# GpSimd adds the two bias rows of output projection and cross attention to the residual rows, in place of VectorE

## The chip, the cores and the metric

One Trainium2 chip, one of its cores. The time is the device time of one launch in microseconds (us); of several runs the median counts.

## The reference, cut to what matters

A decoder of two layers on x, 8 sequences of 256 rows of 256 numbers (fp32). Around the change, in the second layer:

```
x = x + L1_attn_ref(layernorm(x), ...)     # state-space mixer: ... return y @ out_proj_w.T + out_proj_b
x = x + L1_xattn_ref(layernorm(x), ctx)    # cross attention, 8 heads: ... return out @ Wo + bo
x = x + L1_ffn_ref(layernorm(x), ...)      # experts, top 2 of 8
```

out_proj_b and bo are rows of 256 numbers, the same for every row of x. The kernel holds them as `r_out` and `r_xo`, spread over the 128 partitions.

## The kernel before, in words

The 2048 rows lie in four pairs of sequences; a pair is 512 rows, four tiles of 128 rows by 256 numbers. `xst` holds the residual rows of all pairs in SBUF, so the rows of one pair are 128 partitions by 1024 numbers. Every engine runs a queue of its own, in the order in which it is written, and the queues meet at semaphores: `wait_ge` waits, `then_inc` counts up when an instruction is done. `hold` is a wait followed by a semaphore instruction.

After the first layer the function `mixer(p, q, n)` is called six times by `ssm_and_cross` (L157), once per step of a software pipeline over the pairs: n is the pair whose head (similarity, gates and projections up to the step sizes of the state space) is worked on, p the pair in the state space, q the pair in cross attention. The six calls are named M0 to M5 here: M0 is (None, None, 0), M1 (0, None, 1), M2 (1, 0, 2), M3 (2, 1, 3), M4 (3, 2, None), M5 (None, 3, None). M2 and M3 are the two turns of a hardware loop.

Inside one call VectorE's queue is (L1536 to L1593): the first drive product (L1483), then 32 units, each with a scan (L1493), the next unit's drive product (L1483), a piece of the head of pair n and of the cross attention of pair q, and the product that TensorE sums (L1501). Behind the units comes what is called the end here: products with the gate (L1551, L1552), the convolution of pair n (L1510, L1512), then

- the projection of pair p is added to its residual rows from PSUM, in two halves (L1567), and `r_out` is added to the pair's four tiles at once (L1569, counted by `xc_ready`), then the statistics of these rows (L1354, L1357); GpSimd turns the variance into 1/sqrt (L556, L557), and VectorE scales the rows (L1363, counted by `xn_ready`);
- between them the last tile of cross attention of pair q is added (L1474), and `r_xo` is added to the pair's four tiles at once (L1575); the statistics and the scaling of these rows follow, into `xr` (counted by `xr_ready`);
- the step sizes of pair n: the positive part from PSUM (L1585), and `step_sizes` (L1521 to L1534), which wait for ScalarE's absolute values (L994) and exponentials (L998). The last four-unit product L1534 is what the first drive product of the next call waits for.

GpSimd's queue in `mixer` (L644 to L668): the 1/sqrt of each normalisation, a copy of `xr` into `hst` (L663) once `xr_ready` has come, and, once the second half of the step sizes is there (`dt_ready`, L1532), three small memsets of the decay tiles (L668), for which the first drive product also waits (`starts_ready`). GpSimd does larger additions in the first layer too: L597 adds a bias row to a pair, 128x1024, the same shape as the additions above.

SyncE waits for `xc_ready` of all pairs (L528) before it loads the token numbers and the first expert weights. The first tile of cross attention in a pair waits for `xc_ready` as well (L1473).

The quoted lines, from VectorE's queue:

```
v.tensor_tensor(half, proj_banks[s][:, :].rearrange(...), half, ALU.add).then_inc(proj_added, 1)                 # L1567
v.tensor_tensor(pair, pair, wide(r_out, TT), ALU.add).then_inc(xc_ready, 1)                                      # L1569
step.apart(v.tensor_tensor(xst[:, ts(q, TT), :], xst[:, ts(q, TT), :], wide(r_xo, TT), ALU.add))                 # L1575
```

Of the kernel before, what the change touches and what calls it, by code (L numbers as in the profile page):

```python
# [9 lines left out]
ALU = mybir.AluOpType  # L10
# [3 lines left out]
P = 128  # L14
B, S, D = 8, 256, 256
# [3 lines left out]
PAIRS = B // 2  # L19
TT = 4  # L20
# [25 lines left out]
ATTN_STEPS, FFN_STEPS = 4, 12  # L46
BLOCKS, SLOTS = 6, 12
END_STEPS, HEAD_ALONE = 5, 28
HEAD_STEPS, TAIL_STEPS, CROSS_STEPS = 47, 5, 22
ACT_STEPS = 2 * UNITS  # L50
CROSS_SLOTS = 38
ROUTED_EARLY = 36
# [79 lines left out]
def hold(eng, sem, value):  # L132

    eng.wait_ge(sem, value)
    eng.sem_inc(HELD[0], 1)
# [21 lines left out]
def ssm_and_cross(eng, body):  # L157

    body(None, None, 0)
    body(0, None, 1)
    with eng.Fori(0, PAIRS - 2) as r:
        body(r + 1, r, r + 2)
    body(PAIRS - 1, PAIRS - 2, None)
    body(None, PAIRS - 1, None)


def begun(p, q):  # L170


    if p is not None:
        return p + 1, p, 0 if q is None else q
    return (0, 0, 0) if q is None else (PAIRS, PAIRS, q)
# [27 lines left out]
def decoder(nc, t, out):  # L203
    ctx = ExitStack()

    def sem(name):
        return ctx.enter_context(nc.semaphore(name))

    ts = bass.ts
# [5 lines left out]
    xst = keep(NT, D)  # L215
# [48 lines left out]
    r_gf, r_bef, r_out, r_xo = (rows2[:, i * D:(i + 1) * D] for i in range(4))  # L264
# [115 lines left out]
    out_done = sem("out_done")  # L380
    w_cross_in = sem("w_cross_in")
    w_in_2, ctx_in, a_exp, a_ready = sem("w_in_2"), sem("ctx_in"), sem("a_exp"), sem("a_ready")
    xn_ready, xc_ready, xf_kept = sem("xn_ready"), sem("xc_ready"), sem("xf_kept")
    ctxn_in, head_done, head_a, head_v = sem("ctxn_in"), sem("head_done"), sem("head_a"), sem("head_v")
    ge_ready, sil_ready = sem("ge_ready"), sem("sil_ready")
    late_done, late_out, tail_tr = sem("late_done"), sem("late_out"), sem("tail_tr")
# [1 line left out]
    proj_added = sem("proj_added")  # L388
# [8 lines left out]
    route_done, wo2_out = sem("route_done"), sem("wo2_out")  # L397
    u_ready, dtx_ready = sem("u_ready"), sem("dtx_ready")
    at2T_done, at2T_out = sem("at2T_done"), sem("at2T_out")
    xr_ready = sem("xr_ready")  # L400
    soft_e_ready, soft_u_ready, abs_ready, relu_ready = sem("soft_e_ready"), sem("soft_u_ready"), sem("abs_ready"), sem("relu_ready")

    logits_ready, sel_ready, rank_done, lt_ready, gexp_ready, places_ready = (
# [24 lines left out]
    def _(sp):  # L428
# [96 lines left out]
        def slot_tags_in(e, j):  # L525
            sp.dma_start(slot_tags[j], tags_to[ts(e, CAP), :].rearrange("(t p) c -> p t c", p=P)).then_inc(tags_in[j], 16)

        sp.wait_ge(xc_ready, PAIRS)  # L528
        for one in tags:
            sp.dma_start(one, t["tokens"]).then_inc(tokens_in, 16)  # L530
        for j in range(2):
# [18 lines left out]
    def _(pool):  # L550
        step = Steps(pool, pool_step)

        def deviations(n, c, k):

            hold(pool, var_ready, n)
            step.apart(nc.gpsimd.tensor_scalar(ve[:, c:c + k], mv[:, c:c + k, 1], LN_EPS, None, ALU.add))  # L556
            nc.gpsimd.tensor_tensor(rstd[:, c:c + k], ve[:, c:c + k], mhalf[:, 0:k], ALU.pow).then_inc(rstd_ready, 1)  # L557
# [86 lines left out]
        def mixer(p, q, n):  # L644
            heads, tails, ends = begun(p, q)
            groups = 3 * heads + tails + ends
            step.at(groups + 1)
            if p is None and n is None:
                send_rows(0, NT - TT, 1)
            if n is not None and p is not None:  # L650
                for k in range(3):
                    deviations(GROUPS + groups + k + 1, 0, TT)
            more = 3 if n is not None else 0
            if p is not None:
                deviations(GROUPS + groups + more + 1, 0, TT)
                more += 1
            if q is not None:
                deviations(GROUPS + groups + more + 1, 0, TT)
                hold(pool, xr_ready, q + 1)
                if p is None:  # L660
                    pool.sem_inc(xf_kept, 1)
                else:
                    nc.gpsimd.tensor_copy(hst[:, ts(q, TT), :], xr).then_inc(xf_kept, 1)  # L663
            if n is not None:

                hold(pool, dt_ready, 2 * n + 2)
                for one in dA:
                    nc.gpsimd.memset(one.rearrange("p n (s t) -> p (n s) t", s=2)[:, :, 0], 0.0).then_inc(starts_ready, 1)  # L668

        ssm_and_cross(pool, mixer)  # L670

# [369 lines left out]
    def _(dve):  # L1041
        step = Steps(dve, dve_step)
        v = nc.vector
# [288 lines left out]
        def mixer(p, q, n, head_alone=False):  # L1332
            heads, tails, ends = begun(p, q)
# [12 lines left out]
            def wide(r, n):  # L1346
                return r.unsqueeze(1).broadcast_to([P, n, r.shape[1]])

            def rows_of(pair):
                return [xst[:, bass.ds(pair * TT + i, 1), :].rearrange("p a d -> p (a d)") for i in range(TT)]  # L1350
# [104 lines left out]
            def cross(i):  # L1455

                if i % 2 == 0 and i // 2 < 16:
                    u = i // 2
                    dve.wait_ge(s2_done, 16 * q + u + 1)
                    step.after(v.tensor_reduce(mx[:, u % 4, :], at.score[u % 2][:, :].rearrange("p (b j) -> p b j", b=2), AX, ALU.max))  # L1460
                    v.tensor_scalar(nm[:, u % 4, :], mx[:, u % 4, :], -SCALE, None, ALU.mult).then_inc(nm_ready, 1)
                if i % 8 == 0 and i >= 8:
                    tile = i // 8 - 1
                    dve.wait_ge(av2_done, 16 * q + 4 * tile + 4)
                    step.after(v.reciprocal(sm[:, tile, :], sm[:, tile, :]))
                    v.tensor_tensor(at2.rearrange("p (h d) -> p h d", h=QH), bank_av[:, :].rearrange("p (h d) -> p h d", h=QH),
                                    sm[:, tile, :].unsqueeze(2).broadcast_to([P, QH, QD]), ALU.mult).then_inc(at2_ready, 1)
                if i % 8 == 3 + drain and i >= 11 + drain:
                    tile = (i - 11 - drain) // 8
                    row_of = xst[:, bass.ds(q * TT + tile, 1), :].rearrange("p a d -> p (a d)")  # L1470
                    dve.wait_ge(wo2_done, 4 * q + tile + 1)
                    if tile == 0:
                        dve.wait_ge(xc_ready, q + 1)  # L1473
                    v.tensor_tensor(row_of, at.out[:, 0:D], row_of, ALU.add).then_inc(wo2_out, 1)  # L1474

            def drive(i):
# [83 lines left out]
                    end_statistics(PAIRS - 1)  # L1560
                    end_added(PAIRS - 1, GROUPS + 3)
            if p is not None:
                rows, pair = rows_of(p), xst[:, ts(p, TT), :]
                for s in range(2):
                    half = xst[:, bass.ds(p * TT + 2 * s, 2), :]
                    dve.wait_ge(proj_done, 2 * p + s + 1)
                    v.tensor_tensor(half, proj_banks[s][:, :].rearrange("p (t d) -> p t d", t=2), half, ALU.add).then_inc(proj_added, 1)  # L1567
                dve.wait_ge(proj_added, 2 * p + 2)
                v.tensor_tensor(pair, pair, wide(r_out, TT), ALU.add).then_inc(xc_ready, 1)  # L1569
                hold(dve, xc_ready, p + 1)  # L1570
                statistics(rows)
            if q is not None:
                cross(UNITS + 3 + drain)
                dve.wait_ge(wo2_out, 4 * q + 4)
                step.apart(v.tensor_tensor(xst[:, ts(q, TT), :], xst[:, ts(q, TT), :], wide(r_xo, TT), ALU.add))  # L1575
            if p is not None:
                if q is not None:
                    dve.wait_ge(tail_tr, p)
# [748 lines left out]
```

## Time and profile before

| what | value |
|---|---|
| median of 3 runs | 2439.77 us (2437.06 to 2440.63) |
| the profiled execution | 2427.17 us, its span 2425.4 us |
| PE busy in the span | 2075.0 us, 86% |
| VectorE (DVE) busy | 1743.5 us, 72% |
| ScalarE (ACT) busy | 1053.9 us, 43% |
| GpSimd (POOL) busy | 338.5 us, 14% |
| chain that ended last | PE 52%, DVE 32%, issue 10%, ACT 4%, POOL 1% |
| granted TensorE clock, mean | 0.913 |

The span runs from the first to the last instruction of the profiled execution; its own time has 1.8 us more. Engines work beside each other, so busy shares don't add up, and an engine with a small share can still stand in the way at one place.

### The profile page before, as it was taken

To read this page: it belongs to the slowest core of one execution; us is meant where nothing else is said; L and a number is where in the kernel's file an instruction comes from. 1 tells how busy PE (TensorE), PEld (TensorE's weight loads), DVE (VectorE), ACT (ScalarE), POOL (GpSimd) and SP (SyncE) were. 2 spreads that over 40 slices of the span, in tenths; PEclk is the share of its full clock that TensorE was granted. 3 is DMA by queue.
4 is the path that set the end of the run, shared out by engine and by line. 5 is a ranking of instruction groups with operands and counts; after the bars stand their busy time and mean duration, and the time that the engine had idled before them with its cause. 6 is when DMAs were issued, how large, how long until landed. Compare 5 with 4: busy or idle time off the path is not lost.

```text
span 2425.4 us, 33657 instructions
## 1 busy us (share of the span) xinstructions
PE 2075.0 (86%) x12304; PEld 1275.0 (53%) x12304; DVE 1743.5 (72%) x2584; ACT 1053.9 (43%) x1646; POOL 338.5 (14%) x364
## 2 busy tenths in 40 slices
PE   5999999999999999884659787988698888749997
PEld 3666666666666666541224344444344445626665
DVE  6677777777777778769999999989999994120000
ACT  1222222222222222337675867586758861312221
POOL 1111111111111111100000100100010000344222
PEclk8999999999999999997879888988899986659999
DMA  6000000000000100011111111111001103113441
GB/s 237 1 1 18 27 26 1 18 27 26 1 18 13 46 1 1 1 39 58 52 41 36 42 35 42 37 41 35 35 19 59 53 18 109 43 35 94 117 115 17
DMA packets 62428, 99.24 MB, mean 41 GB/s; under 512 B 13268, under 2 KB 45039, under 8 KB 61776
## 3 DMA queue, kind: packets, MB, share of 16 engines
q1 hardware_dynamic: 55120, 90.10, 11.2%
q0 software_dynamic: 7168, 7.32, 1.7%
q8 instruction: 83, 1.36, 0.2%
q14 instruction: 57, 0.47, 0.1%
HBM read 83.01 MB, written 15.53 MB: 41 GB/s over the span
## 4 chain that ended last, share of the span: by engine, by line
PE 52%; DVE 32%; issue 10%; ACT 4%; POOL 1%; DMA 1%; DVEq 0%; ACTq 0%; POOLq 0%; SPq 0%
PE po L1728 9%; PE pa L1718 9%; DVE arena L1493 8%; PE pa L2258 5%; PE po L2267 5%; PE pa L1676 4%; DVE arena L1483 4%; PE pt L1693 3%; PE pa L1998 2%; DVE arena L1115 2%; DVE arena L1501 2%; PE pa L1708 2%; PE po L2037 2%; PE pa L1767 1%; DVE arena L1117 1%
## 5 line engine op out<-in xcount | busy, mean ns | idle before, releaser
L1998 PE MATMUL pa<-arena 128*128 128x512 f32 x512 | 298.5, 712 | 87.8 <-DVE arena L1501 87.6
L1493 DVE TENSOR_TENSOR_SCAN arena<-arena 128x1024 f32<-128x1024 f32 x128 | 292.3, 2283 | 7.9 <-ACT arena L899 7.5
L556 POOL TENSOR_SCALAR arena<-arena 128x2 f32<-128x2 f32 (+1 forms) x92 | 27.7, 301 | 1513.3 <-DVE arena L1357 836.2
L1728 PE MATMUL po<-arena 128*128 128x256 f32 x960 | 224.2, 385 | 0.0
L1998 PEld LDWEIGHTS pa<-arena 128*128 128x128 f32 x512 | 101.2, 217 | 219.0 <-DVE arena L1501 117.6
L1718 PE MATMUL pa<-arena 128*128 128x512 f32 x480 | 212.3, 594 | 3.6 <-ACT arena L719 3.3
L1185 DVE TENSOR_TENSOR arena<-pa,arena 128x512 f32<-128x512 f32 x256 | 158.5, 681 | 68.2 <-PE pa L1676 68.2
L741 ACT COPY arena<-pa 128x512 f32<-128x512 f32 x128 | 65.7, 600 | 325.3 <-PE pa L1676 325.3
L883 ACT ACTIVATE arena<-arena 128x510 f32<-128x510 f32 x256 | 170.5, 717 | 59.5 <-DVE arena L1493 51.3
L1728 PEld LDWEIGHTS po<-arena 128*128 128x128 f32 x960 | 176.7, 189 | 32.9 <-issue 6.0
L1621 DVE TENSOR_TENSOR arena<-po,arena 128x512 f32<-128x512 f32 x16 | 11.1, 692 | 236.9 <-PE po L2267 236.9
L1655 PE MATMUL po<-arena 128*128 128x128 f32 x440 | 79.5, 312 | 105.0 <-ACT arena L925 73.8
L1483 DVE TENSOR_TENSOR arena<-arena 128x1024 f32<-128x1024 f32 x128 | 154.8, 1209 | 8.5 <-PE pa L1998 5.7
L1501 DVE TENSOR_TENSOR arena<-arena 128x1024 f32<-128x1024 f32 x128 | 155.7, 1217 | 0.3
L1718 PEld LDWEIGHTS pa<-arena 128*128 128x128 f32 x480 | 89.9, 189 | 116.5 <-issue 116.2
L894 ACT ACTIVATE arena<-arena 128x1020 int16<-128x1020 f32 x128 | 145.4, 1136 | 1.1 <-ACT arena L883 0.7
L1676 PE MATMUL pa<-arena 32*128 32x128 f32 x3072 | 129.6, 289 | 11.0 <-ACT arena L728 5.5
L1655 PEld LDWEIGHTS po<-arena 128*128 128x128 f32 x440 | 55.4, 159 | 155.1 <-ACT arena L925 106.6
L1676 PEld LDWEIGHTS pa<-arena 32*128 32x128 f32 x3072 | 107.5, 191 | 51.1 <-issue 35.5
L899 ACT ACTIVATE arena<-arena 128x1020 f32<-128x1020 int16 x128 | 133.6, 1044 | 0.2
L728 ACT ACTIVATE arena<-pa,arena 128x512 f32<-128x512 f32 x120 | 82.2, 687 | 98.4 <-PE pa L1718 98.2
L1767 PE MATMUL pa<-arena 128*128 128x512 f32 x256 | 118.3, 616 | 5.1 <-issue 4.3
(247 smaller groups left out, 3739.6 us busy)
## 6 DMA issues: line engine op xcount, KB each, us to landing
arena<-bc_rows SPq DMA_DIRECT2D x64, 512.0 KB, 4.3
arena<-in_L_ffn_W SPq DMA_DIRECT2D x16, 1024.0 KB, 8.0
arena<-in_L_attn_W SPq DMA_DIRECT2D x8, 1024.0 KB, 5.6
rows_to_experts<-arena SPq DMA_DIRECT2D x4, 1024.0 KB, 12.7
arena<-rows_to_experts SPq DMA_DIRECT2D x8, 512.0 KB, 9.7
out<-arena SPq DMA_DIRECT2D x5, 512.0 KB, 8.9
arena<-in_x SPq DMA_DIRECT2D x4, 512.0 KB, 5.9
arena<-in_rows SPq DMA_DIRECT2D x8, 256.0 KB, 3.1
```

The source lines that it names most:

```text
L883: last = a_(past_start(dA[i % len(dA)])[:, 2 * n:2 * n + 2, :], dt[:, c, :].rearrange("p (s t) -> p s t", s=2)[:, :, 1:], ACT.Exp, scale=a ...
L894: return step.mark(a_(past_start(steps16[i % 2]), past_start(dA[i % len(dA)]), ACT.Relu, scale=-DECAY_STEPS, bias=const[:, C_MID:C_MID + 1]))
L1185: v.tensor_tensor(scm[:, (4 * block + g) % SLOTS, :, :], pa[g][:, :].rearrange("p (h q) -> p h q", h=4), tri.unsqueeze(1).broadcast_to([P, ...
L1483: v.tensor_tensor(uh[i % len(uh)], dtx[:, c, :].unsqueeze(1).broadcast_to([P, NG, W]), Bs[g % 2], ALU.mult).then_inc(u_ready, 1)
L1493: v.tensor_tensor_scan(h.rearrange(flat), decay.rearrange(flat), h.rearrange(flat), 0.0, ALU.mult, ALU.add).then_inc(scan_done, 1)
L1501: v.tensor_tensor(h, h, Cs[g % 2], ALU.mult).then_inc(hc_ready, 1)
L1655: return nc.tensor.transpose(dst, src, ident)
L1676: last = mm(pa[g][:, ts(e, P)], keys, qf[ts(g, 32), c, ts(rows_of, P)], start=True, stop=True)
L1718: last = mm(pa[(i + 2) % 4][:, :], w1[:, k, ts(i, P)], yT[:, k, :], start=k == 0, stop=k == KC - 1)
L1728: last = mm(po[s][:, ts(i, D)], gT[:, c, ts(tile, P)], w2[:, c, :], start=c == 0, stop=c == FM - 1)
L1767: last = mm(pa[(j + 2) % 4][:, :], (wq if j < KC else wk)[:, k, ts(j % KC, P)], hT[:, k, :], start=k == 0, stop=k == KC - 1)
L1998: last = mm(pa[c][:, :], ident, uh[i % len(uh)][:, n, :], start=g == 0 and n == 0, stop=g == NS // NG - 1 and n == NG - 1)
```

## The change

VectorE no longer adds `r_out` (L1569) and `r_xo` (L1575). In each `mixer` call GpSimd adds `r_out` to the residual rows of pair n behind its three memsets, and `r_xo` to the rows of pair p once these have been scaled (`xn_ready`), behind its copy for pair q and ahead of its wait for the step sizes. So there are four additions of each kind, in M0 to M3 for `r_out` and in M1 to M4 for `r_xo`. VectorE waits for `r_out_added` ahead of L1567 and for `r_xo_added` at the first tile of cross attention. SyncE's wait goes by `proj_added`.

```
-HEAD_STEPS, TAIL_STEPS, CROSS_STEPS = 47, 5, 22
+HEAD_STEPS, TAIL_STEPS, CROSS_STEPS = 47, 5, 21
...
-        sp.wait_ge(xc_ready, PAIRS)
+        sp.wait_ge(proj_added, 2 * PAIRS)
...
                     nc.gpsimd.tensor_copy(hst[:, ts(q, TT), :], xr).then_inc(xf_kept, 1)
+
+            def biased(pair, bias, done):
+                rows = xst[:, ts(pair, TT), :]
+                nc.gpsimd.tensor_tensor(rows, rows, bias.unsqueeze(1).broadcast_to([P, TT, D]), ALU.add).then_inc(done, 1)
+
+            if p is not None:
+                hold(pool, xn_ready, 3 * heads + tails + (3 if n is not None else 0) + 1)
+                biased(p, r_xo, r_xo_added)
             if n is not None:
 
                 hold(pool, dt_ready, 2 * n + 2)
                 for one in dA:
                     nc.gpsimd.memset(one.rearrange("p n (s t) -> p (n s) t", s=2)[:, :, 0], 0.0).then_inc(starts_ready, 1)
+                biased(n, r_out, r_out_added)
...
                     if tile == 0:
-                        dve.wait_ge(xc_ready, q + 1)
+                        dve.wait_ge(r_xo_added, q + 1)
...
             if p is not None:
-                rows, pair = rows_of(p), xst[:, ts(p, TT), :]
+                rows = rows_of(p)
+                dve.wait_ge(r_out_added, p + 1)
                 for s in range(2):
...
                     v.tensor_tensor(half, proj_banks[s][:, :].rearrange("p (t d) -> p t d", t=2), half, ALU.add).then_inc(proj_added, 1)
-                dve.wait_ge(proj_added, 2 * p + 2)
-                v.tensor_tensor(pair, pair, wide(r_out, TT), ALU.add).then_inc(xc_ready, 1)
-                hold(dve, xc_ready, p + 1)
+                hold(dve, proj_added, 2 * p + 2)
                 statistics(rows)
             if q is not None:
                 cross(UNITS + 3 + drain)
-                dve.wait_ge(wo2_out, 4 * q + 4)
-                step.apart(v.tensor_tensor(xst[:, ts(q, TT), :], xst[:, ts(q, TT), :], wide(r_xo, TT), ALU.add))
+                if p is None:
+                    hold(dve, wo2_out, 4 * q + 4)
+                else:
+                    dve.wait_ge(wo2_out, 4 * q + 4)
```

## Rows read from the trace of the kernel before

**Rows 1.** Busy time per engine in the units of M1 (stretch, its length, then each engine).

```profile
core 0: us, PE busy (x) PEld busy (x) DVE busy (x) ACT busy (x) POOL busy (x), PEclk, DMA share, GB/s
1113.30:1284.60 171.30, 106.05 (x210) 42.98 (x211) 169.68 (x170) 117.48 (x146) 11.28 (x6) 0.78 0.13 42
```

**Rows 2.** VectorE's waits in M2, the longest (total us, times, longest).

```profile
DVE arena L1474 <- PE pt L2123: 5.7, 2, 3.6
```

**Rows 3.** Single lines: durations ns min/median/max, first and last start us.

```profile
L1569 DVE TENSOR_TENSOR arena<-arena x4: 1224/1225/1227, 1300.9 to 2010.6; 128x1024 f32<-128x1024 f32 x2, 128x1024 f32 x2
...
L1575 DVE TENSOR_TENSOR arena<-arena x4: 1224/1224/1225, 1548.4 to 2131.1; 128x1024 f32 x2, 128x1024 f32<-128x1024 f32 x2
...
L597 POOL TENSOR_TENSOR arena<-arena x16: 2356/2366/2395, 25.2 to 952.8; 128x1024 f32<-128x1024 f32 x16
...
L1161 DVE TENSOR_TENSOR_SCAN arena<-arena x64: 657/660/1616, 34.1 to 956.8; 128x256 f32<-128x256 f32 x64
...
L663 POOL COPY arena<-arena x3: 1037/2945/2960, 1558.0 to 2023.0; 128x1024 f32 x2, 128x1024 f32<-128x1024 f32 x1
```

**Rows 4.** Timeline, first layer: GpSimd's addition beside VectorE (start us, us, engine, line).

```profile
952.63 1.53 DVE L1154 SCALAR_TENSOR_TENSOR arena<-pa,arena 128x512 f32<-128x512 f32 x2
...
952.82 2.36 POOL L597 TENSOR_TENSOR arena<-arena 128x1024 f32<-128x1024 f32 x1
954.19 2.12 DVE L1161 TENSOR_TENSOR_SCAN arena<-arena 128x256 f32<-128x256 f32 x2
```

**Rows 5.** Timeline of the end of M2.

```profile
1543.27 0.68 DVE L1567 TENSOR_TENSOR arena<-pa,arena 128x512 f32 x1
...
1548.42 1.22 DVE L1575 TENSOR_TENSOR arena<-arena 128x1024 f32 x1
1548.65 1.88 POOL L557 TENSOR_TENSOR arena<-arena 128x4 f32<-128x4 f32 x1 [0.18 <-POOL arena L556]
1550.57 1.38 DVE L1363 TENSOR_SCALAR arena<-arena 128x256 f32 x4 [0.92 <-POOL arena L557]
...
1554.40 1.04 POOL L557 TENSOR_TENSOR arena<-arena 128x4 f32<-128x4 f32 x1 [0.18 <-POOL arena L556]
1555.49 2.00 ACT L998 ACTIVATE arena<-arena 128x1024 f32<-128x1024 f32 x2
...
1557.61 1.28 DVE L1521 TENSOR_SCALAR arena<-arena 128x1024 f32<-128x1024 f32 x2
...
1557.98 2.94 POOL L663 COPY arena<-arena 128x1024 f32 x1 [2.54 <-DVE arena L1363]
1558.81 1.22 DVE L1522 TENSOR_SCALAR arena<-arena 128x2048 f32<-128x2048 f32 x1
1560.06 3.01 DVE L1524 SCALAR_TENSOR_TENSOR arena<-arena 128x2048 f32<-128x2048 f32 x1
```

**Rows 6.** Timeline of the entry into M1.

```profile
1112.04 1.23 DVE L1534 TENSOR_TENSOR arena<-arena 128x1024 f32<-128x1024 f32 x1
1112.16 0.18 POOL L668 MEMSET arena<- 128x4 f32 x3 [23.61 <-DVE arena L1532]
...
1113.30 1.23 DVE L1483 TENSOR_TENSOR arena<-arena 128x1024 f32<-128x1024 f32 x1
```

**Rows 7.** Timeline: first drive product of M2 and of M3, first projection half of M3.

```profile
1327.93 1.23 DVE L1483 TENSOR_TENSOR arena<-arena 128x1024 f32<-128x1024 f32 x1 [0.25 <-DVE arena L1534]
...
1577.82 1.23 DVE L1483 TENSOR_TENSOR arena<-arena 128x1024 f32<-128x1024 f32 x1 [2.56 <-issue]
...
1794.53 0.68 DVE L1567 TENSOR_TENSOR arena<-pa,arena 128x512 f32 x1
```

**Rows 8.** Timeline of the end of M1.

```profile
1307.20 2.72 DVE L1585 TENSOR_SCALAR arena<-pa,arena 128x512 f32<-128x512 f32 x4
...
1310.49 0.69 DVE L1521 TENSOR_SCALAR arena<-arena 128x1024 f32<-128x1024 f32 x1 [0.57 <-ACT arena L998]
...
1313.30 2.29 DVE L1524 SCALAR_TENSOR_TENSOR arena<-arena 128x2048 f32<-128x2048 f32 x1
```

**Rows 9.** Timeline of the end of M4.

```profile
2016.51 1.38 DVE L1363 TENSOR_SCALAR arena<-arena 128x256 f32<-128x256 f32 x4 [1.01 <-POOL arena L557]
```

More of the change, by code:

```diff
@@ L382, in decoder @@
     w_in_2, ctx_in, a_exp, a_ready = sem("w_in_2"), sem("ctx_in"), sem("a_exp"), sem("a_ready")
-    xn_ready, xc_ready, xf_kept = sem("xn_ready"), sem("xc_ready"), sem("xf_kept")
+    xn_ready, xf_kept = sem("xn_ready"), sem("xf_kept")
     ctxn_in, head_done, head_a, head_v = sem("ctxn_in"), sem("head_done"), sem("head_a"), sem("head_v")
@@ L399, in decoder @@
     at2T_done, at2T_out = sem("at2T_done"), sem("at2T_out")
-    xr_ready = sem("xr_ready")
+    xr_ready, r_out_added, r_xo_added = sem("xr_ready"), sem("r_out_added"), sem("r_xo_added")
     soft_e_ready, soft_u_ready, abs_ready, relu_ready = sem("soft_e_ready"), sem("soft_u_ready"), sem("abs_ready"), sem("relu_ready")
```

## The prediction

> **What bounds the kernel here.** I read the page first (which engines are busy, and where), then the busy time of the stretches M0 to M5, then VectorE's waits in them, and last the timeline of each end and entry. In the units of M1 VectorE is busy 169.68 of 171.30 us [rows 1]: whatever makes its queue longer there makes the kernel longer. In M2 it waits a few times for TensorE, most of all at the cross rows [rows 2]. So the change is worth what it does to VectorE's queue between about 1110 and 2140 us; the first layer and the experts are not touched.
>
> **What is removed.** Four L1569 and four L1575, 1.22 us each [rows 3], 9.8 us of VectorE's work. How much of it lies on the path is worked out below, end by end.
>
> **What is added.** Eight additions of 128x1024 on GpSimd. The nearest row is the same shape on the same engine, L597 with 2.37 us [rows 3]. GpSimd has the time; the question is what the additions do to VectorE beside them. Three rows show it. The scan L1161 takes 0.66 us, at most 1.62 [rows 3]; the long one begins at 954.19 while GpSimd's addition runs until 955.18, and the pair of scans needs 2.12 us [rows 4]: the first stood 0.96 us, until the addition was over. The L1154, which take one operand from PSUM, keep their pace beside the same addition [rows 4]. And the copy L663, 1.04 us alone [rows 3], takes 2.94 in M2: it starts at 1557.98, gets nowhere while L1521 and L1522 run (until 1560.03), ends 0.89 us later, and L1524, which should start at 1560.06, takes 3.01 us [rows 5] instead of 2.29 [rows 8]. So these two engines shut each other out when VectorE's instruction has all its tensors in SBUF; the one that waits gets in where VectorE's next instruction waits for a result; and it then holds VectorE up until it is nearly done.
>
> I call x what one addition costs VectorE in such a place. Worked out from the copy: of 1.04 us, 0.89 came after it got in and 0.72 hit VectorE, so 0.15 and 0.17 fall away, and 2.37 leaves 2.05 to 2.2. I take **x = 2.1**. Its bounds are 0 (it is never let in at a bad moment) and 2.37 (all of it counts). The Trainium skill (SBUF — State Buffer, Who interferes with whom) says that a VectorE instruction with two SBUF inputs and a GpSimd instruction that reads SBUF exclude each other for the whole instruction, the one that started first winning; by that x would be the whole 2.37 and the sum below 1.3 us higher. It speaks against this change, and no row contradicts it.
>
> **The additions of r_out, at the entries.** GpSimd is released by L1532, does its memsets at 1112.16 and would start the addition about 0.3 us later. L1534 then runs until 1113.27, and the first drive product starts at 1113.30 because it waits for L1534 [rows 6]. That is the moment at which the copy got in ahead of L1524. The drive product has two inputs in SBUF, so it starts x later, and the whole chain of units behind it. In M1 nothing can take this up [rows 1]: **+2.1**. The entries into M2 (L1483 at 1327.93 [rows 7]) and into M4 have the same order: **+2.1 each**. At the entry into M3 VectorE's queue stands 2.56 us by itself ahead of the drive product ("issue", the turn of the loop) [rows 7]; the addition fits in there: **0**, and it would be another x if that pause went. Three entries: +6.3.
>
> **The additions of r_xo, and what is saved, at the ends.**
> - M1: L1521 waited 0.57 us for ScalarE's exponentials [rows 8], and these hang on TensorE's chain, not on L1569. The saved 1.22 us become waiting: **0**. The new addition runs beside L1585, which reads PSUM [rows 8], and is over before L1521: **0**. Were that cover gone, it would be x.
> - M2: two things shorten the way to the first L1363: L1569 with its gap (1.25 us) and GpSimd's L557, which took 1.88 us beside L1575 and takes 1.04 without it [rows 5]. But ScalarE's exponentials end at 1557.49 [rows 5] in any case, so L1521 to L1522 can't end before 1559.3, 0.7 earlier than they did. The copy now comes about 1.3 us sooner and falls into L1521's wait between its halves, where it costs some 0.6; so L1522 ends at about 1559.9. The new addition has queued behind the copy and gets in there, as the copy did before, and L1524 starts at 1559.9 + 2.1 = 1562.0. In the run of before it effectively started at 1560.06 + 0.72 = 1560.78. **+1.2**, that is x - 0.9.
> - M3 is the same code with the same pattern: **+1.2**.
> - M4: no head, so nothing hides the statistics: L1363 waits for L557 [rows 9], and TensorE for L1363. Both savings count, 1.25 + 0.85: **-2.1**. The addition of r_xo runs when VectorE has nothing to do: 0.
> - M5: L1575 stands alone between the last cross row and the router: **-1.25**. GpSimd adds nothing here.
>
> New waits: GpSimd's for `xn_ready` has always been met when it is reached behind the copy; behind it queue the memsets, but `dt_ready` comes only after all of the step sizes, which VectorE begins at L1521 [rows 5], so they aren't late. VectorE's two new waits look at additions of the call's own entry and of the call before: 0. SyncE's token and weight loads start 1.2 us sooner, far ahead of their users: 0.
>
> **Sum**: 3x + 2(x - 0.9) - 3.35 = 5x - 5.15; with x = 2.1 it is +5.35. To this an echo: M3's first drive product came 2.3 us later than it would have without its pause, and from there to L1567 M3 needed 216.71 us, M2 215.34 (from 1327.93 to 1543.27) [rows 5, 7]. A late start wasn't made good, it cost 1.4 more. M2 will now start late in the same way; I take half, +0.7. In all **+6.0 us**: the profiled execution of 2427.17 us would become 2433.2. It lies 12.6 below the median of the runs, which are the measure, so 2439.8 + 6.0 = **2445.8**. About 0.2%, 4.9 us, is what a measurement can tell from no change.
>
> **Rivals.**
> - *The additions slip in at no cost.* Place: the entries, 0.03 us wide at 1113.27 [rows 6]. If GpSimd isn't let in there and gets its turn beside VectorE's statistics or its PSUM reads, x is near 0 and only the savings are left: 0 + 2(-0.9) - 3.35 = -5.15, 2434.6 us. It decides below x = 1.03, where the sum turns negative, and counts as faster only near 0. Against it: the copy got in across a gap just as small [rows 5]. Chance 0.13.
> - *Late starts are made good.* In M2 and M4 VectorE waits for TensorE now and then, 5.7 us at L1474 in M2 [rows 2]. If these waits shrink, the entries of M2 and M4 are free: 2.1 + 2.4 - 3.35 = +1.2, 2441.0 us. Against it: M3's echo. Chance 0.17.
> - *The late starts cost TensorE its clock.* If all three entries echo with the full 1.4 and the savings of M4 are eaten by slow matmuls, it is 5.35 + 4.2 + 2.1 = +11.7, 2451.4 us. Chance 0.12.
> - My forecast has 0.58; within it x and the echo leave about a third below 4.9 us.
>
> **How the numbers follow.** Slower by over 0.2%: two thirds of 0.58, plus 0.12, is 0.51. Faster by over 0.2%: of the first rival most, 0.11. The rest, 0.38, is within 0.2%. The range reaches down to x = 0.4 (about 2436.7) and up to the third rival (2451.5); what it leaves out at the two ends is under 2 in 10. The forecast's own range is 2443 to 2449.
>
> **What would show it.** After the change, L1483 at the entries of M1, M2 and M4 lasting about 3.3 us instead of 1.23; the new GpSimd additions lasting over 3 us there and 2.4 in M1's and M4's ends; L1524 in M2 and M3 at over 4 us; L557 at 1.04 us at the ends; L1521 in M1 waiting longer than 0.57. The prediction is wrong if L1483 keeps 1.23 us at the entries, if M2's units are shorter by what the entry lost, or if the end of M2 shows L1521 no longer bound by L998.

## The result and the profile after

The changed kernel takes 2473.31 us (median of 4 runs, 2470.46 to 2478.62), the kernel before 2440.20 us beside it (2437.06 to 2443.89): a ratio of **1.0127, with a 95% interval of 1.0113 to 1.0141**. By that ratio it is slower by 31 us; the two medians themselves lie 33.1 us apart. The forecast was 6 us slower, with a range that ended at 2451.5.

The page of the kernel after (most lines of VectorE and ScalarE are 9 higher than before, TensorE's 10; L1567 became L1577, L1592 became L1602; the end's L1521 to L1534 became L1530 to L1543; GpSimd's memset L668 became L676, and its new addition is L667):

```profile
span 2470.5 us, 33666 instructions
...
PE 2105.6 (85%) x12304; PEld 1287.9 (52%) x12304; DVE 1746.8 (71%) x2576; ACT 1053.5 (43%) x1646; POOL 354.2 (14%) x372
```

VectorE has eight instructions fewer and is still busy 3 us longer; TensorE has the same 12304 matmuls and is busy 30.6 us longer. So the first thing to look for is slower matmuls, not a longer queue.

**Entries.** Timeline of the entry into M1, kernel after, VectorE and GpSimd (start us, us, engine, line), to be held against [rows 6]:

```profile
1113.13 1.23 DVE L1543 TENSOR_TENSOR arena<-arena 128x1024 f32<-128x1024 f32 x1
1114.39 3.25 DVE L1492 TENSOR_TENSOR arena<-arena 128x1024 f32<-128x1024 f32 x1
...
1113.25 0.17 POOL L676 MEMSET arena<- 128x4 f32 x3 [24.61 <-DVE arena L1541]
1113.38 3.18 POOL L667 TENSOR_TENSOR arena<-arena 128x1024 f32<-128x1024 f32 x1
```

The addition is recorded from 1113.38 and stands until L1543 is over at 1114.36, gets in at the 0.03 us in which VectorE waits, and VectorE's drive product lasts 3.25 instead of 1.23 us: 2.02 us more. The same is seen at the entry of M2 (3.04 us) and of M4 (3.25 us), not at that of M3 (1.23 us).

**Ends.** Timeline of the end of M2, kernel after, beside [rows 5]:

```profile
1563.79 1.37 DVE L1372 TENSOR_SCALAR arena<-arena 128x256 f32 x4
1565.49 4.31 DVE L1530 TENSOR_SCALAR arena<-arena 128x1024 f32<-128x1024 f32 x2 [0.33 <-ACT arena L1007]
1569.72 1.22 DVE L1531 TENSOR_SCALAR arena<-arena 128x2048 f32<-128x2048 f32 x1
1570.97 2.29 DVE L1533 SCALAR_TENSOR_TENSOR arena<-arena 128x2048 f32<-128x2048 f32 x1
...
1565.45 1.04 POOL L663 COPY arena<-arena 128x1024 f32 x1 [3.21 <-DVE arena L1372]
1566.45 2.79 POOL L667 TENSOR_TENSOR arena<-arena 128x1024 f32 x1
```

The copy L663 is back at 1.04 us, and the addition behind it holds up the second half of L1530 (the pair takes 4.31 us where L1521 took 1.28), one instruction earlier than the prediction had it (L1524, now L1533). From L1577 to the last step size M2's end is 1.29 us longer, M3's 1.25 us.

**Where the 31 us arise.** I took the same milestones (first drive product, first scan, last scan, first projection half, router product of each call) from the timelines of both profiled executions and put the differences against the kernel before in a table: how much longer each step took.

| step | predicted | measured |
|---|---|---|
| entries of M1, M2, M3, M4 | +2.1, +2.1, 0, +2.1 | +2.02, +1.82, +0.22, +2.02 |
| ends of M1, M2, M3, M4 | 0, +1.2, +1.2, -2.1 | 0, +1.29, +1.25, -2.80 |
| units of M1 (first scan to last) | 0 | 0 |
| units of M2, M3, M4 | +0.7 in all | +3.95, +3.24, +6.16 |
| M5 (router of M4 to router of M5) | -1.25 | +5.85 |
| all else up to M5's router, most of it ahead of M1 | 0 | +1.2 |
| behind M5's router (the experts) | 0 | +18.9 |

The steps from M1's entry to M5's router make 25.0 us. The 18.9 us behind them are another matter, and no part of the change; nor do the 25.0 us reach the 31 of the ratio, and no row places the last 6. ScalarE's waits in the experts, kernel after (us in total, times, longest):

```profile
ACT arena L1046 <- remote: 27.1, 4, 9.8
```

ScalarE stands up to 9.8 us at a time for something that the profile calls remote (another core or an unknown queue) and that no row explains. Such stands (up to 10.5 us at a time, 9 to 28 us in all) are in this profile and in the eight that were taken on the two chips where the kernel before had a median of 2442 us, also in kernels with nothing changed near them (late_1, late_3). They are in none of the seven profiles from the two chips where it had 2424 us, and not in the profile of before that the prediction used, which fits its lying 12.6 us under its median. With them the part behind M5's router takes 291 to 305 us, without them 279 to 282. Below it is left out of the comparison, and ratios compare kernels on the same chip.

**TensorE.** The units of M2, M3 and M4, and M5, in both kernels (stretch, its length, PE busy with the count of matmuls, granted clock, DMA share, GB/s). Before:

```profile
1329.30:1543.30 214.00, 172.39 (x580) 0.88 0.10 34
1579.20:1794.50 215.30, 173.02 (x576) 0.87 0.09 31
1827.80:2006.40 178.60, 145.85 (x490) 0.91 0.11 38
2035.10:2143.90 108.80, 84.37 (x328) 0.61 0.09 32
```

After:

```profile
1334.20:1552.20 218.00, 174.97 (x575) 0.86 0.10 33
1589.60:1808.20 218.60, 176.40 (x575) 0.85 0.08 31
1844.70:2029.60 184.90, 152.82 (x485) 0.85 0.11 37
2055.50:2170.10 114.60, 94.74 (x328) 0.56 0.09 31
```

In M5 the same 328 matmuls take 10.4 us more at a mean granted clock of 0.56 instead of 0.61. In M2 to M4 the levels are lower by 0.02 to 0.06, and in the four stretches together PE is busy 23.3 us more. So most of the excess is TensorE's clock, and what remained was why it falls.

### The profile page after: what moved, and what is told of

Same layout as the page of the kernel before. It is cut to its first block, busy times and chain, and to the rows that moved or that the text cites. A ratio compares the mean times of both kernels' runs of the same rounds, so it can differ in the third digit from the quotient of the medians.

```text
span 2470.5 us, 33666 instructions
## 1 busy us (share of the span) xinstructions
PE 2105.6 (85%) x12304; PEld 1287.9 (52%) x12304; DVE 1746.8 (71%) x2576; ACT 1053.5 (43%) x1646; POOL 354.2 (14%) x372
## 3 DMA queue, kind: packets, MB, share of 16 engines
q8 instruction: 83, 1.36, 0.2%
## 4 chain that ended last, share of the span: by engine, by line
PE 53%; DVE 29%; issue 10%; ACT 4%; another core or an unknown queue 1%; DMA 1%; POOL 1%; DVEq 0%; ACTq 0%; SPq 0%; POOLq 0%
PE po L1738 9%; PE pa L1728 8%; DVE arena L1502 8%; PE po L2277 5%; PE pa L1686 4%; PE pa L2268 4%; DVE arena L1492 4%; PE pt L1703 3%; PE pa L2008 3%; DVE arena L1124 2%; DVE arena L1510 2%; PE po L2047 2%; PE pt L2019 1%; PE pa L1718 1%; DVE arena L1126 1%
## 5 line engine op out<-in xcount | busy, mean ns | idle before, releaser
L1502 DVE TENSOR_TENSOR_SCAN arena<-arena 128x1024 f32<-128x1024 f32 x128 | 292.4, 2284 | 10.8 <-ACT arena L908 10.4
L1492 DVE TENSOR_TENSOR arena<-arena 128x1024 f32<-128x1024 f32 x128 | 160.8, 1256 | 10.9 <-PE pa L2008 7.8
L1510 DVE TENSOR_TENSOR arena<-arena 128x1024 f32<-128x1024 f32 x128 | 155.9, 1218 | 0.3
L1686 PE MATMUL pa<-arena 32*128 32x128 f32 x3072 | 129.4, 288 | 10.5 <-ACT arena L737 5.5
```

Of the source, the lines that this page charges most:

```text
L1492: v.tensor_tensor(uh[i % len(uh)], dtx[:, c, :].unsqueeze(1).broadcast_to([P, NG, W]), Bs[g % 2], ALU.mult).then_inc(u_ready, 1)
L1502: v.tensor_tensor_scan(h.rearrange(flat), decay.rearrange(flat), h.rearrange(flat), 0.0, ALU.mult, ALU.add).then_inc(scan_done, 1)
L1510: v.tensor_tensor(h, h, Cs[g % 2], ALU.mult).then_inc(hc_ready, 1)
L1686: last = mm(pa[g][:, ts(e, P)], keys, qf[ts(g, 32), c, ts(rows_of, P)], start=True, stop=True)
```

## The experiments

Fifteen runs in four groups; before_again and after_again repeat a kernel, the other thirteen are new kernels. Each group had its own runs of the kernel before on the same chip: median 2424 us in the first and last group, 2442 in the second and third. The times in the first group's expectations were reckoned from 2440, so ratios are what can be held against them.

**before_again**: the kernel before, unchanged, to see how much two executions of one kernel differ.

> The kernel before, unchanged, for a second profile. Its first profiled execution (2427.2 us) lay 12.6 us under the median of its other runs, that of the changed kernel on its median. Theory A (the first experts' stalls are a matter of the execution, not of the change): this profile shows the first expert (from its first up projection to its last down projection) longer than the 30.6 us of the first profile, by up to 12. Rival: they come with the change; then it is 30.6 us again.

Measured: 2422.76 us, ratio 0.9997 (0.9988 to 1.0007). The longer first expert that I expected wasn't there, on a chip of the other kind; that such stands come without the change too was shown only by the second group. And the stretches differ from those of the first profile: units of M2 +2.13, M3 +1.35, M4 -3.27, M5 -3.84 us. Later profiles differ more: M3's units lie between -2.09 and +4.74 us in late_1, late_3 and last_only, which change nothing in M1 to M3 but the time at which they begin. So a single stretch of a single profile says little within 4 to 7 us; the tables below are read with that in mind.

**xo_only, out_only, neither**: the change taken apart.

```
xo_only:  -                biased(n, r_out, r_out_added)              (GpSimd)
          +  VectorE adds r_out behind the projection, as before
out_only: -                biased(p, r_xo, r_xo_added)                (GpSimd)
          +  VectorE adds r_xo behind the cross rows, as before
neither:  both biased() calls gone, VectorE adds nothing either
```

> r_xo on GpSimd, r_out back on VectorE. Theory A (the loss enters where GpSimd's r_out addition holds up the first drive product, and grows in the units behind it): 2440 to 2445 us, the first drive products 1.23 us again, the ends of M2 and M3 longer by 1 to 3 us. Rival B (each blocked addition is worth some 6 us, wherever it stands): 2452 us or more.

> r_out on GpSimd, r_xo back on VectorE. Theory A: most of the loss, 2462 to 2475 us, the first drive products of M1, M2 and M4 at 3.0 to 3.3 us. Rival B: about 2455 us.

> No engine adds the two bias rows (the kernel leaves these additions out; all other work, the waits included, is that of the changed kernel). Theory A: the savings alone, 2433 to 2438 us. Rival C (it isn't the additions, but the changed waits or the moved code): well above 2445 us without any addition.

Measured: xo_only 1.0068 (1.0050 to 1.0086), out_only 1.0098 (1.0080 to 1.0117), neither 1.0044 (1.0028 to 1.0060). The local steps came cleanly apart: entries +2.0, +1.8 and +2.0 in out_only alone and 0 in the others; ends of M2 and M3 +1.46 and +1.45 in xo_only, -0.88 and -0.90 in out_only, -0.87 and -0.90 in neither. The striking one is neither. It only takes work away, and is 0.44% slower: its M5 takes 5.29 us more than before, at a clock of 0.55. Whatever costs that time needs no GpSimd. (I had expected the savings to show.) The kernel doesn't compute the two biases.

**after_again, late_1, late_3, spots.** The first is the changed kernel once more. late_1 and late_3 are the kernel before with one and with three repeated products at M0's end, so that everything from M1 on comes 1.25 or 3.75 us later. spots puts GpSimd's r_xo where VectorE isn't held up, and VectorE's r_out in M4 ahead of the projection, where VectorE waits anyway.

```
late_k (k = 1 or 3), shortened, in step_sizes, ahead of the last dtx product of M0:
+    for extra in range(k):
+        v.tensor_tensor(dtx[:, half], dt[:, half], xs[:, half], ALU.mult).then_inc(late_start, 1)
+        dve.wait_ge(late_start, extra + 1)
spots, VectorE, ahead of the projection:
+    if n is None:
+        v.tensor_tensor(pair, pair, wide(r_out, TT), ALU.add).then_inc(r_out_added, 1)
```

> The changed kernel once more, for its ratio beside the other kernels and for a second profile. Theory A (26 us of the first profile come from the mixer, 20 us from stalls of ScalarE in the first expert that belong to that execution or chip): 2446 to 2456 us, and the first expert needs some 32 us again instead of 52. Rival: the stalls belong to the change; then 2465 us or more, with ScalarE standing several us at a time in the first expert.

> The kernel before, but VectorE writes the second half of dtx once more in M0 (the same product again): its first drive product of M1 comes 1.25 us later, nothing else changes. Theory T (what a kernel loses in the units of M2 to M5 hangs on where TensorE's clock happens to be at its lower level, and any shift in time changes that): 1.25 us and something else, between -4 and +9 us against before, with the same two-valued unit times (unit 4: 9.3 or 11.9 us, unit 29: 4.8 or 6.5 us) in another pattern. Rival S (each late start is simply handed on, or grows in proportion): +1.25 us, at most +2.

> As late_1, but three more products, 3.75 us. Theory T: not three times the difference of late_1; 0 to +13 us. Rival S: +3.75 us, at most +6.

> r_xo on GpSimd, but ahead of the 1/sqrt of the cross rows, where VectorE has instructions with one SBUF operand; r_out on VectorE, in M4 ahead of the projection, where it waits for TensorE. By the terms of my sum: 2 x -0.7 (M2, M3), -2.1 (M4), -1.25 (M5), -4.7 us or 2419 us. Theory T: the terms show in the stretches where they arise, and the whole may still be off by some 5 us to either side. Rival S: 2419 us within 1.5.

Measured: after_again 1.0112 (1.0069 to 1.0155), late_1 1.0015 (1.0003 to 1.0028), late_3 1.0027 (1.0012 to 1.0042), spots 1.0039 (1.0028 to 1.0051). A shift of everything costs what is added, or a few us more: 3.7 us (0.7 to 6.8) for 1.25, and 6.6 (2.9 to 10.3) for 3.75. Both intervals are too wide to tell my theory from its rival. spots was expected at -4.7 us and is 9.5 us slower: it had its local steps as meant (ends of M2 and M3 -0.7, M4 -3.16) and lost them in M5, +5.51. after_again again had ScalarE's stands in the first expert, 9.2 us, which my rival took for a sign of the change; late_1 and late_3 have 23.2 and 27.9 us of them. And after_again repeats the changed kernel's stretches in M3, M4 and M5 within 0.3 us (M2 within 1.2), where two executions of before differ by 1.4 to 3.8: the loss is not an accident of one execution.

**late_all, late_entries, after_late, last_only**: is it the lateness or the additions?

```
late_entries, from before: a repeated product and one of half its size (1.95 us) ahead of the
  first drive product of M1, M2 and M4
late_all, from neither: the same, and two repeats of L1531 (2.2 us; the second of three
  quarters) in the ends of M2 and M3; no biases
after_late: the changed kernel with late_1's product
last_only, from before: in M4 r_out ahead of the projection, GpSimd adds r_xo of the last pair
```

> No engine adds the two biases; instead repeated VectorE instructions make VectorE late at the places and by about the amounts at which the changed kernel was late: about 1.95 us at the entries of M1, M2 and M4, and 2.2 us at the ends of M2 and M3. No addition on GpSimd anywhere. If lateness alone makes the rest of the loss, whatever engine causes it, this takes what the changed kernel takes: ratio 1.010 to 1.013, M4's units and M5 some 6 us longer each than before. If the additions do something more to TensorE or VectorE in the units, it stays at +4 to +5 us from the delays, ratio 1.001 to 1.004.

> The kernel before, with the first drive products of M1, M2 and M4 about 1.95 us late by repeated products; nothing else touched. The queue alone: +5.9 us, ratio 1.0024. If late starts at several entries cost TensorE its clock: +10 us or more, ratio 1.005 to 1.010, near that of the kernel with r_out alone on GpSimd (1.0098). If late starts are made good: below 1.0015.

> The changed kernel with one more repeated product at the end of M0: everything from M1's first drive product on is 1.25 us later. By the queue alone +1.25 us on the changed kernel, so 1.013 to 1.014 against the kernel before. If the loss in M4 and M5 is a matter of how the waits and matmuls happen to fall in time, these stretches change by several us either way and the ratio can lie anywhere from 1.007 to 1.016.

> A candidate: only the last two calls are changed. In M4 VectorE adds r_out ahead of the projection, where it waits for TensorE, and GpSimd adds r_xo beside it; M5 has no bias addition. M1 to M3 are the kernel before to the instruction. By the queue alone: M4's end 2.9 us shorter, M5 1.25 us shorter, -4.1 us, ratio 0.9983. If TensorE's clock answers any shift of M5 with a loss as in the kernel in which nothing is added (M5 +5.3 us): +1 us, ratio 1.0005.

Measured: late_all 1.0089 (1.0067 to 1.0110), late_entries 1.0077 (1.0049 to 1.0104), after_late 1.0118 (1.0092 to 1.0143), last_only 1.0011 (0.9999 to 1.0023). How much longer than in before the units took:

| kernel | M2 | M3 | M4 | what makes VectorE late |
|---|---|---|---|---|
| after, after_again, after_late | +3.95, +5.12, +4.78 | +3.24, +3.49, +3.27 | +6.16, +6.19, +6.14 | GpSimd |
| late_all | +5.15 | +3.25 | +2.34 | repeated instructions |
| late_entries | +5.40 | +1.36 | +3.68 | repeated instructions |
| before_again, late_1, late_3 | +2.13, -1.27, -0.04 | +1.35, +4.74, -2.09 | -3.27, -3.18, -1.53 | (nothing at the entries of M2 to M4) |

Some single stretches are within what kernels with nothing late show, the sum of the three isn't: taken over all 17 profiles, those of the last group below included, it lies between -3.7 and +4.9 us in the nine where nothing is late from M2 to M4 (the three of the last row, neither, spots, last_only, neither_padded, short_end, and before itself), and between +5.9 and +14.8 in the eight where something is (out_only +5.9, xo_only +8.4, after_padded +10.2, and the five of the first three rows).

late_entries has 5.85 us of extra work and is 18.8 us (0.77%; 12 to 25) slower. (In the profiles, up to M5's router, it is 16.0.) So starting VectorE 2 us late at three places costs two to four times what it weighs, with no GpSimd in it. That is no fixed factor: late_all has 10.25 us more work than neither and is 11 us slower by the two ratios. It missed the 1.010 that I had set as its lower bound, and its M4 and M5 didn't get 6 us longer each. after_late speaks against its being a matter of when in the run it happens: 1.25 us later, the changed kernel's pattern is the same. last_only gained nothing, although its M5 wasn't longer (-0.60). My expectation for its M4 was also wrong: r_xo of the third pair stays on VectorE there, and M4's end shrank by 1.04 us, not 2.9.

How the lateness turns into slow matmuls is seen in the first units of M4. Timeline of TensorE (start us, us, line, idle before it and what ended it), kernel before:

```profile
1829.04 1.10 PE L2009 MATMUL pt<-arena 64*128 64x256 f32 x4 [0.99 <-ACT arena L870]
1830.07 1.13 PE L2059 MATMUL po<-arena 128*128 128x512 f32 x2
1831.12 1.12 PE L2060 MATMUL po<-arena 64*128 64x512 f32 x2
1832.40 1.99 PE L1998 MATMUL pa<-arena 128*128 128x512 f32 x4
```

Kernel after:

```profile
1842.45 1.10 PE L2019 MATMUL pt<-arena 64*128 64x256 f32 x4 [1.63 <-ACT arena L879]
1843.48 1.64 PE L2069 MATMUL po<-arena 128*128 128x512 f32 x2
1845.05 2.07 PE L2070 MATMUL po<-arena 64*128 64x512 f32 x2
1849.34 3.78 PE L2008 MATMUL pa<-arena 128*128 128x512 f32 x4 [2.22 <-DVE arena L1510]
```

late_entries:

```profile
1841.06 1.12 PE L2071 MATMUL po<-arena 64*128 64x512 f32 x2
1844.32 3.78 PE L2009 MATMUL pa<-arena 128*128 128x512 f32 x4 [2.14 <-DVE arena L1506]
```

TensorE's matmuls for the head and cross attention don't wait for the entry, so it runs dry: where it went from L2060 to L1998 almost without a stop, it now stands 2.2 us for VectorE, and the four matmuls then take 3.78 us instead of 1.99, at the lower of the two clock levels (1.2 instead of 2.4 GHz). But the stand isn't the whole of it. The granted clock ahead of it (PE busy, clock, DMA share, GB/s), kernel after and then late_entries:

```profile
1840.50:1843.95 3.45, 1.82 (x6) 1.00 0.42 140
1843.95:1847.12 3.17, 3.17 (x4) 0.50 0.00 0
...
1840.40:1843.65 3.25, 1.78 (x4) 1.00 0.00 0
1843.70:1847.10 3.40, 2.78 (x4) 0.50 0.00 0
```

In late_entries the clock falls in the stand. In the changed kernel it has fallen 3.2 us before the stand begins (L2070 already takes 2.07 us instead of 1.12), after a stop of 1.63 us for ScalarE where before had 0.99. The 17 profiles fall into groups by what is late. The clock falls 0.7 to 0.9 us ahead of M4's first scan where both M3's end and M4's entry are longer (after, after_again, after_late, after_padded, late_all), 1.0 us behind it where only the end is (xo_only), 4.0 and 4.9 us behind it where only the entry is (late_entries, out_only), and 9.9 to 12.8 us behind it in the nine others. VectorE pays for it; kernel after, at the third scan of M4,

```profile
1858.45 2.29 DVE L1502 TENSOR_TENSOR_SCAN arena<-arena 128x1024 f32<-128x1024 f32 x1 [3.17 <-ACT arena L908]
```

it waits 3.17 us for ScalarE. Before, the third scan had no wait, and the second had waited 2.73 us (0.66 after): so the late start is made good in the second unit, and more than lost again in the third. Most units keep their time to 0.1 us; a few have two or three values. In before, before_again and late_1, M4's units 1 and 2 take 7.3 and 5.3 us, unit 4 5.3 to 5.5; in after, after_again, after_late, late_all and late_entries they take 5.2 to 5.4, 8.2 to 9.0 and 6.7. In the first three of these, and not in the two that imitate them, units 13 to 15 take another 3.8 us more than in before. This second part can't be put down to late starts alone: units 13 to 15 are 3.0 us longer in neither too, where nothing is late, and not in neither_padded, which has the same code up to there. The Trainium skill (TensorE: Matmul & The Clock Gate, Part 1: The HAM clock gate) says that the array runs at either of two clocks, by how busy it has been; the rows agree, with 1.00 or 0.50 granted and 1.99 or 3.78 us for the same four matmuls.

**after_padded, neither_padded, short_end**: what sets M5? Over the runs so far M5 took 104.9 to 109 us or 114 to 116 us, and the long form went with an end of M4 that was shorter by 1.14 us or more, in all kernels but late_all. The experiments give M4's end its old length by work of no use, or take it away in the kernel before.

```
after_padded and neither_padded, VectorE in M4, where L1569 and L1575 stood:
+    v.tensor_tensor(rows, rows, rows, ALU.max).then_inc(padded, 1)
+    dve.wait_ge(padded, count)
short_end, from before: r_out of the last pair, r_xo of the last two pairs are not added
```

> The changed kernel with M4's end made as long as before by two VectorE instructions of the same size (maxima of rows with themselves) where the two bias additions stood; nothing else touched. If shortening M4's end is what puts M5's matmuls into low clock: M5 takes some 104 to 108 us instead of 114.6, the granted clock in it is 0.61 or more instead of 0.56, and the kernel gets about 3 us faster than the changed one although 2.5 us of work were added (ratio about 1.011). If M5's clock comes from elsewhere: M5 stays at 114.6 and the kernel gets 2.7 us slower than the changed one (ratio 1.014).

> The kernel in which nothing adds the two biases, with the same two instructions in M4's end. If the shorter end of M4 is the cause: M5 from 114.1 to some 104 to 108 us, in all about 4 us faster than without the two instructions, ratio about 1.002. Otherwise 2.6 us slower than it, ratio about 1.0055.

> The kernel before without the two bias additions in M4's end and the one in M5 (three fewer VectorE instructions, output incomplete); M1 to M3 untouched. By the queue alone: M4's end 2.7 us and M5 1.25 us shorter, -3.9 us, ratio 0.9984. If the shorter end of M4 puts M5 into low clock: M5 gets 5 to 6 us longer instead, at a clock of 0.56, and the kernel is 2 to 3 us slower, ratio 1.001.

Measured: after_padded 1.0080 (1.0066 to 1.0094), neither_padded 1.0021 (1.0011 to 1.0030), short_end 1.0036 (1.0022 to 1.0050). All three went the way of the theory that M4's end sets M5's clock: two instructions more, and the kernel without the biases is faster (1.0044 to 1.0021) and the changed one too (1.0127 and 1.0112 to 1.0080); three fewer, and the kernel before is slower, beside it on one chip. The changed kernel itself was never timed on a chip of the 2424 us kind, so its pair compares ratios from chips of both kinds; in the profiles M5's router comes 12.4 us sooner. M4's end is given against before:

| kernels | M4's end | M5, us | clock in M5 |
|---|---|---|---|
| before, before_again, late_1, late_3, late_entries, xo_only | -0.40 to +0.16 | 104.9 to 109.0 | 0.61 to 0.65 |
| after_padded, neither_padded | -0.07, 0.00 | 103.8, 104.1 | 0.65 |
| last_only | -1.04 | 108.2 | 0.62 |
| out_only | -1.14 | 116.2 | 0.55 |
| after, after_again, after_late | -2.80 each | 114.6, 114.7, 114.3 | 0.56 |
| neither, spots, short_end | -2.60, -3.16, -3.03 | 114.1, 114.3, 115.7 | 0.54 to 0.56 |
| late_all | -2.60 | 106.8 | 0.61 |

All fit but late_all, and why I can't say. Between -1.04 and -1.14 there is hardly a difference, so the length alone is not the whole of it. late_all begins M5 as the long ones do, but has the full clock for 20 us from 62 us on, where they have it for 3.4 us at most. M5 cut into three stretches (columns as above), after_padded:

```profile
2053.90:2089.90 36.00, 31.79 (x109) 0.51 0.02 8
2089.90:2125.90 36.00, 28.73 (x143) 0.82 0.15 51
2125.90:2157.70 31.80, 19.54 (x80) 0.62 0.12 43
```

After:

```profile
2055.50:2091.50 36.00, 32.26 (x108) 0.50 0.02 8
2091.50:2127.50 36.00, 32.42 (x114) 0.59 0.11 40
2127.50:2170.10 42.60, 30.06 (x110) 0.58 0.12 41
```

short_end:

```profile
2036.50:2072.50 36.00, 32.22 (x108) 0.50 0.02 9
2072.50:2108.50 36.00, 32.01 (x110) 0.59 0.11 40
2108.50:2152.20 43.70, 31.51 (x113) 0.54 0.12 40
```

The first 36 us are at the low level in all three, and in before. Then after_padded has the full clock for most of 36 us and gets 143 matmuls through; after and short_end have it for short pieces only and get 114 and 110. Which matmuls pay is seen by shape, in M5 of the kernel before (mean ns, then idle before):

```profile
L2037 PE MATMUL po<-arena 128*128 128x64 f32 x128 | 28.0, 391 | 14.5 <-ACT arena L935 14.5
L2009 PE MATMUL pt<-arena 64*128 64x256 f32 x60 | 24.9, 553 | 0.3 <-DVE arena L1592 0.3
...
L2123 PE MATMUL pa<-arena 128*128 128x256 f32 x32 | 11.3, 515 | 0.7 <-ACT arena L938 0.7
```

and after:

```profile
L2019 PE MATMUL pt<-arena 64*128 64x256 f32 x60 | 29.7, 643 | 0.3 <-DVE arena L1602 0.3
L2047 PE MATMUL po<-arena 128*128 128x64 f32 x128 | 28.9, 400 | 11.1 <-ACT arena L944 10.1 <-issue 1.0
...
L2133 PE MATMUL pa<-arena 128*128 128x256 f32 x32 | 14.6, 639 | 0.7 <-ACT arena L947 0.7
```

The wide ones pay, 4.8 and 3.3 us of the 10.4; the 64-column ones, which wait between for ScalarE, hardly do, and 3.4 us less of their idle time gives part of it back. Net M5 is 5.85 us longer, although L1575's 1.22 us are gone.

after_padded and neither_padded, timed beside each other, also give the price of GpSimd's additions with M5 out of it. They make the entries of M1 to M4 and the ends of M2 and M3 9.9 us longer in all, and the kernel 14.3 us slower by the ratios (14.5 us up to M5's router in the profiles): 1.4 times their own length.

No version beat the kernel before; the nearest with the whole computation was last_only, at 1.0011.

## Why the prediction was right in direction and wrong in size

- **Exclusion, x = 2.1.** Right. The additions cost VectorE 2.02, 1.82 and 2.02 us at the three entries, and M3's pause in the loop took up the fourth (+0.22, as in before_again). The Trainium skill's rule (SBUF — State Buffer, Who interferes with whom) would have the addition cost its whole 2.37 us. No entry did: at M1 L667 ended 2.20 us after L1543 had let it in, and 2.02 of these hit VectorE. That the two exclude each other the runs bear out.
- **L1524 as the victim in M2 and M3.** Wrong instruction, right cost: the addition got in at L1530's wait between its halves. +1.29 and +1.25 against +1.2. In xo_only it was +1.46, and without the additions -0.9; the prediction's bound for what could be saved there was 0.7.
- **M1's end 0.** Right: L1530 now waits 1.62 us for ScalarE where it waited 0.57 [rows 8], and nothing moved.
- **M4's end -2.1.** Right for VectorE's part: from the first L1577 to the first L1372 it was -2.11, with L557 at 1.04 us as predicted. It was -2.80 in all, since TensorE's stretch from the last L1372 to the router also took 0.72 us less.
- **M5 -1.25.** Failed, by 7.1 us. The saved instruction was the only effect I looked for. Nothing in that step asked what the 2.8 us saved just before would do to TensorE's clock.
- **The echo, +0.7.** This is the term that failed most. I had one instance (M3, 1.4 us) and took half of it once. That instance was no echo: M3's units were longer than M2's by 1.3 us there, by 0.6 in before_again and 7.4 in late_1, and shorter by 0.6 in late_3. The units of M2, M3 and M4 took 3.95, 3.24 and 6.16 us more, 13.4 in all. Since executions of before differ in the same stretches by 2 to 4 us, not each number is the change's; the sum is beyond the -3.7 to +4.9 us of kernels with nothing late, and late_entries, with 18.8 us for 5.85 us of work, shows the size without GpSimd.
- **The direction.** The terms of VectorE's queue alone came out at 4.6 us (entries 6.1, ends -0.3, L1575 -1.2) against 5.35. They are small beside 31 us, so the direction came out right by a sum that held little of what happened.
- **The rival "late starts cost TensorE its clock"** named the mechanism that decided, with 0.12 and +11.7 us. Its price came from 1.4 us for each entry and 2.1 for M4. Measured are 13.4 us in the units, and M5 7.1 us off. And slow matmuls came even where nothing is late (neither, short_end), so "late" was too narrow: M5's part comes with M4's end being short.
- **"Slip in free"** and **"made good"** are refuted by the drive products of 3.25 us and by units that got longer in sum.

Shown by intervention: lateness of VectorE, with no GpSimd in it, costs more than its length in late_entries (two to four times), and the length of M4's end moves M5's level in three trials out of three. Only seen together: that the clock falls sooner at the start of M4 the more is late there. Open: how the length of M4's end acts on levels that differ only some 40 us into M5; late_all's M5; what decides whether units 13 to 15 of M4 are slow; why M2's units took only 0.63 us more in after_padded, whose code there is the changed kernel's; why neither_padded, with less work than before and a short M5, is still 0.21% slower; and some 6 of the 31 us.

## What to carry to other kernels

Where TensorE's granted clock stands between its levels for a whole stretch (0.61 in M5 here), cost an edit near it not by its own microseconds alone but by what it does to TensorE's gaps, and give the range the difference between such a stretch at the one and the other level; two executions of the unchanged kernel show how much of that is there already. An instruction moved to an idle engine is not free at the moment where it becomes ready: look for the next place where the busy engine waits, even for 0.03 us, since that is where it gets in. And a kernel that only has work taken away (neither) tells more than the parts of the change do: if it isn't faster, the work was not what cost the time.

## What was unexpected in the hardware

- Removing three VectorE additions made a kernel 0.36% slower (short_end), and adding two instructions of no use made others faster, 1.0044 to 1.0021 and 1.0112 or 1.0127 to 1.0080. In both M5 changed by 7 to 11 us with the same 328 matmuls (95.74 and 80.05 us of TensorE's time).
- The granted clock fell from 1.00 to 0.50 though TensorE had stood no longer than 1.63 us (kernel after, ahead of M4's units), in a stretch in which it had been busy 1.82 of 3.45 us.
- The pattern is repeated to 0.4 us in M3 to M5 in three profiles of the changed kernel, one of them with 1.25 us added ahead of M1, and yet differs by 3.8 us between two profiles of the kernel before.
- On some chips ScalarE stood up to 10.5 us at a time in the experts, 9 to 28 us in all, whatever the kernel; the medians of the kernel before differ by 16 to 18 us between such chips and the others (2440 to 2442 and 2424).
